# Feed-forward stage: the shared expert's last three down steps moved between the next batch's up steps

## What is computed

```python
shared = jax.nn.silu(x @ shared_w_gate.T) * (x @ shared_w_up.T) @ shared_w_down.T
shared = shared * jax.nn.sigmoid(x @ shared_gate_w.T)
...
out = expert_out + shared
...
x = x + _L0_ffn_ref(_layernorm(x, axis=-1), ...)
```

## Time and profile before

| what | value |
|---|---|
| median of three runs | 855.08 us |
| the profiled execution, its own time | 858.7 us |
| its span | 857.0 us |
| TensorE busy, share of the span | 750.3 us, 88% |
| VectorE busy | 523.9 us, 61% |
| ScalarE busy | 401.4 us, 47% |
| GpSimd busy | 359.9 us, 42% |
| mean granted clock of TensorE | 0.951 |

### The profile page before, as it was taken

How to read it: one execution, slowest core, us unless ns; L and a number is a source line. 1 busy time by engine, 2 the same in 40 slices (tenths; PEclk the granted TensorE clock), 3 DMA queues, 4 the chain that set the end, 5 groups by cost and what they waited for, 6 DMA issues and landing times. The chain is left out here.

```text
span 857.0 us, 16360 instructions
## 1 busy us (share of the span) xinstructions
PE 750.3 (88%) x5618; PEld 569.0 (66%) x5619; DVE 523.9 (61%) x1158; ACT 401.4 (47%) x777; POOL 359.9 (42%) x658
## 2 busy tenths in 40 slices
PE   2589899999999999999887587989679999999997
PEld 1355466575666656666454367868579999988886
DVE  6267777677776768766670349445634445456667
ACT  3116656546655556646556132433435556542232
POOL 4305437283472835625374023767700000057771
PEclk9879999999999999999887868999979999999999
DMA  5659366483755738466111221877645555467864
GB/s 148 236 211 321 143 222 224 167 296 130 250 194 209 261 124 282 138 242 228 61 59 51 86 74 62 301 238 240 239 158 155 181 183 160 134 203 242 265 200 137
DMA packets 102500, 159.67 MB, mean 186 GB/s; under 512 B 7712, under 2 KB 78368, under 8 KB 98208
## 3 DMA queue, kind: packets, MB, share of 16 engines
q1 hardware_dynamic: 96288, 141.99, 49.6%
q0 software_dynamic: 6144, 16.79, 5.7%
HBM read 86.66 MB, written 71.83 MB: 185 GB/s over the span
## 5 line engine op out<-in xcount | busy, mean ns | idle before, releaser
L609 DVE TENSOR_REDUCE neg_max<-ps_w 128x1 f32<-128x512 f32 (+3 forms) x352 | 201.0, 633 | 67.5 <-PE ps_w L711 67.3
L546 ACT ACTIVATE probs<-ps_w 128x512 f32<-128x512 f32 x320 | 167.5, 610 | 32.2 <-PE ps_w L724 31.3
L408 POOL TENSOR_TENSOR pool_scratch<-minus_half 1x1 f32<-1x1 f32 x190 | 34.8, 183 | 263.7 <-ACT probs L546 223.6
L1091 POOL DMA_INDIRECT ex<-yg_dram,slots x64 | 64.5, 1009 | 155.6 <-DMA yg_dram<-y 136.4
L438 POOL TENSOR_SCALAR_AFFINE_SELECT probs<-probs 128x256 f32<-128x256 f32 (+1 forms) x224 | 93.7, 429 | 0.0
L1079 POOL DMA_INDIRECT xg_dram<-srow,slots x64 | 68.0, 1063 | 52.2 <-DVE slots L1242 27.4
L735 PE MATMUL ps_w<-probs,v_aug 128*32 128x512 f32 (+3 forms) x1024 | 81.2, 460 | 5.9 <-POOL probs L438 5.8
L191 PE MATMUL ps_f<-stacks 128*128 128x512 f32 x176 | 72.5, 412 | 12.2 <-DVE xT_lo_f L1260 6.8
L1108 ACT ACTIVATE silu<-ps_f 128x512 f32<-128x512 f32 (+1 forms) x48 | 28.5, 594 | 103.7 <-PE ps_f L193 103.7
L192 PE MATMUL ps_f<-xT_lo_f,stacks 128*128 128x512 f32 x176 | 70.9, 403 | 0.0
L193 PE MATMUL ps_f<-stacks 128*128 128x512 f32 x176 | 70.6, 401 | 0.0
(11 more groups left out here) (167 smaller groups left out, 1839.6 us busy)
## 6 DMA issues: line engine op xcount, KB each, us to landing
qk_dram<-projected SPq DMA_DIRECT2D x96, 256.0 KB, 4.3
stacks<-qk_dram SPq DMA_DIRECT2D x16, 1024.0 KB, 6.1
xg_dram<-zeros SPq DMA_DIRECT2D x20, 512.0 KB, 10.5
srow<-xg_dram SPq DMA_DIRECT2D x40, 256.0 KB, 2.8
q_st<-qk_dram SPq DMA_DIRECT2D x8, 1024.0 KB, 4.8
k_st<-qk_dram SPq DMA_DIRECT2D x8, 1024.0 KB, 8.1
projected<-experts SPq DMA_DIRECT2D x16, 384.0 KB, 4.5
yg_dram<-projected SPq DMA_DIRECT2D x20, 256.0 KB, 2.2
```

Source lines behind the costliest of these rows:

```text
L408: ticks = Ticks(pool, pool_ticks, lambda: pool.tensor_tensor(out=pool_scratch[:, 0:1], in0=minus_half[0:1, 0:1], in1=minus_half[0:1, 0:1], ...
L546: act.activation(probs[:, g, p * PAIR + half * BANK:p * PAIR + (half + 1) * BANK], ps_w[:, plan.bank(kind, which, half), :], ACT.Exp).then ...
L609: dve.tensor_reduce(out=neg_max[u][:, qt, first:first + len(heads)], in_=bank[:, 0:len(heads) * width].rearrange("p (h n) -> p h n", h=len ...
L1091: pool.indirect_dma_start(out=back[:, m, c, :], out_offset=None, in_=yg_rows, in_offset=bass.IndirectOffsetOnAxis(ap=slots[:, c, m:m + 1], ...
```

## The change

Of batches 0, 1, 2 and 4, 5, 6 only down steps 0 to 2 stay behind the batch's own up steps. Steps 3 to 5 stand behind up steps 0, 1 and 2 of the next batch. The four sums of the batch then stand on VectorE behind step 4 of the next batch (`add_down`, `SUMS_BEHIND`), and TensorE's wait for `y_done` keeps its place, ahead of down step 0. The last batch of each half does all its down steps and sums at its end, as before. The low part of the next input (`split_xT`) moves up on both engines to the head of step 6. `x1` gets a second buffer for batches 5 and 7 (`srow[:, 1]`). SyncE stores the sums of batch b-1 and reloads `x1` behind the fifth expert of batch b, or at step 4 of batches 5 and 6. Batch 6's sums aren't stored and read back any more; routed results are added to them in place, and `TILES_BESIDE` moves one tile from batch 4 to batch 7.

```diff
-TILES_BESIDE = {4: (0, 1, 1, 1, 1, 1, 2), ..., 7: (1, 1, 1, 1, 1, 1, 1)}
+TILES_BESIDE = {4: (0, 1, 1, 1, 1, 1, 1), ..., 7: (0, 1, 1, 1, 1, 4, 0)}
+AHEAD = 3
+SUMS_BEHIND = AHEAD + 1
...
+    def x1_of(b):
+        return srow[:, 1] if b > FIRST and b % 2 else x1
...
         def load_x1(b):
-            sp.wait_ge(x1_left, 16 * b)
+            sp.wait_ge(x1_left, 16 * (b if b <= FIRST else b - 1))
...
+        def store_y1(b):
+            sp.wait_ge(y_done, TB * (b + 1))
+            sp.dma_start(item(y1_v, b), x1_of(b)).then_inc(x1_left, 16)
...
         def first_half(b, more):
             load_next_xn(b, more)
             if b == 0:
                 sp.wait_ge(slots_ready, 1)
-            load_x1(b)
+                load_x1(b)
             for e in range(EXPERTS_FROM[b], EXPERTS_FROM[b + 1]):
...
                 if e % 2 and e // 2 < B - 2:
                     rows_of(e // 2 + 2)
-            sp.wait_ge(y_done, TB * (b + 1))
-            sp.dma_start(item(y1_v, b), x1[:, :, :]).then_inc(x1_left, 16)
+                if b and e == EXPERTS_FROM[b] + SUMS_BEHIND:
+                    store_y1(b - 1)
+                    load_x1(b)
+            if not more:
+                store_y1(b)
...
         def second_half(b, more):
-            load_x1(b)
             if b == FIRST:
+                load_x1(b)
+                load_x1(b + 1)
...
+                if FIRST < b < B - 1 and j == SUMS_BEHIND:
+                    store_y1(b - 1)
+                    load_x1(b + 1)
+                    load_y1(b - 1)
...
@@ VectorE @@
+                if j == FT and more:
+                    split_xT(b + 1)
                 if j > 0:
                     dve.wait_ge(h_hi_done, n)
...
-                if j >= 1:
+                if 1 <= j < FT:
                     beside(j - 1)
+                if j == SUMS_BEHIND and b not in (0, FIRST):
+                    add_down(b - 1)
                 if b == 0:
                     routing(j)
+            beside(FT - 1)
...
-            if more:
-                split_xT(b + 1)
             beside(FT)
-            dve.wait_ge(x1_in, 16 * (b + 1))
+            if not more:
+                add_down(b)
...
@@ TensorE @@
             pe.wait_ge(xT_split, (b + 1) * DK)
             for j in range(FT):
-                pe.wait_ge(h_done, b * FT + max(j - 1, 0))
...
+                up(b, j)
...
+                if b not in (0, FIRST) and j + AHEAD < FT:
+                    down(b - 1, j + AHEAD)
...
             pe.wait_ge(y_done, b * TB)
...
-            for j in range(FT):
...
+            for j in range(AHEAD if more else FT):
+                down(b, j)
```

More of the change, by code:

```diff
@@ L908, in build_ffn @@
     stage_in, w_hi_done, w_split = [sem("stage_in0"), sem("stage_in1")], sem("w_hi_done"), sem("w_split")
-    xn_in, x1_in, x1_left = sem("xn_in"), sem("x1_in_f"), sem("x1_left")
+    xn_in, x1_in, x1_left = sem("xn_in"), [sem(f"x1_in_f{n}") for n in range(2)], sem("x1_left")
     xT_ready, xT_hi_done, xT_split = sem("xT_ready"), sem("xT_hi_done"), sem("xT_split")
@@ L952, in fours_loop, with sums_of @@
         four_pairs(TILE_PAIRS - FOUR, False)
+    def x1_of(b):
+        return srow[:, 1] if b > FIRST and b % 2 else x1
+    def sums_of(b):
+        return staged[b % 2] if b < B - 2 else x1_of(b)
     def expert(e, part, lo, hi):
@@ L1420, in ranks, with up, down @@
             pe.matmul(ps[:, COUNT_BANK, :], ones[:, :], flat, start=True, stop=True).then_inc(counts_ready, 1)
+        def up(b, j):
+            pe.wait_ge(h_done, b * FT + max(j - 1, 0))
+            for i in range(2 if j < FT - 1 else 1):
+                col = (2 * j + i) * P
+                for k in range(DK):
+                    at = slice(k * 2 * FF + col, k * 2 * FF + col + P)
+                    last = exact_product(pe, ps[:, 2 + 2 * (j % 2) + i, :], (up_hi[:, at], up_lo[:, at]), (xT_hi[:, k, :], xT_lo[:, k, :]),
+                                         start=k == 0, stop=k == DK - 1)
+            last.then_inc(up_ready, 1)
+        def down(b, j):
+            pe.wait_ge(h_split, b * FT + j + 1)
+            for t in range(TB):
+                last = exact_product(pe, ps[:, 6 + t // 2, (t % 2) * D:(t % 2 + 1) * D],
+                                     tuple(v[0:width(j), j, t * P:(t + 1) * P] for v in (h_hi, h_lo)),
+                                     tuple(v[0:width(j), j * D:(j + 1) * D] for v in (down_hi, down_lo)),
+                                     start=j == 0 and t % 2 == 0, stop=j == FT - 1 and t % 2 == 1)
+                if j == FT - 1 and t % 2:
+                    last.then_inc(down_ready, 1)
         def shared(b, more):
@@ L1442, in shared @@
                 pe.wait_ge(m_y, TILE_PAIRS)
-            for j in range(FT):
[L1444 to L1447, removed]
-                                         tuple(v[0:width(j), j * D:(j + 1) * D] for v in (down_hi, down_lo)),
-                                         start=j == 0 and t % 2 == 0, stop=j == FT - 1 and t % 2 == 1)
-                    if j == FT - 1 and t % 2:
-                        last.then_inc(down_ready, 1)
+            for j in range(AHEAD if more else FT):
+                down(b, j)
         def experts_of(q):
```

52 lines of the change are left out of this document (22 added, 30 removed).

## The result

| | before | after |
|---|---|---|
| median of the runs, us | 855.39 (853.25 to 858.61, 4 runs) | 871.19 (865.81 to 872.72, 4 runs) |
| ratio, 95% interval | | 1.0158 (1.0112 to 1.0204) |
| the profiled execution, us | 858.7 | 871.3 |
| its span, us | 857.0 | 869.6 |
| start of the middle, us | 624.86 | 629.66 |

The changed kernel is slower by 1.6%. (That ratio compares the fast runs of both kernels; the two medians by themselves are 1.8% apart.) The two traces differ by 12.6 us: + 4.8 in the first half, - 0.7 in the middle, + 8.45 in the second half, which begins with batch 4's first up step (752.63 us before, 756.78 after). (The medians differ by 15.8; the profiled execution of before was its slowest one, and I leave the rest to the spread of the executions.)

The account below looks back on a forecast made before the run. Bounds: GpSimd's scatters in the first half, TensorE in the second. The second half's 9.1 us and first half's 1.1 sum to 10.2, which on the 855.08 us median gives 865.3 us; 8-in-10 range 857.5 to 870.

Parts of the forecast that it names:

- the second half: Batches 4 to 7: TensorE is the bound, so new waits, later tail and change of shape cost 9.1 us.
- the first half: Up to the middle's start: 1.1 us later, at 626.0, set by the chain through the last expert's load.
- The wait for the sums in batches 5 and 6: Ahead of down step 0, TensorE waits 2.6 us per batch for VectorE's four sums, 5.2 us in all.
- t: Start of VectorE's product 4 in a batch; sums were forecast from t + 2.24 to t + 3.90.
- The tail of batch 7: From product 4 to the last sums: four more sums and two more tiles on VectorE, 3.7 us more.
- The change of shape: Second half, TensorE: moved steps alternate matmuls of 256 and 512 columns more often, costing 0.2 us.
- The chain: First half's end: expert 13's split, sums, store, last expert's load and splits, batch 3's sums, pair loads; 15.5 us.
- the scatters' gain: First half, GpSimd: by the scatters alone the middle would start 4.9 us earlier; forecast as lost to the chain.
- The scatters decide: Rival, chance 0.22: GpSimd's scatters set the middle's start, 4.9 us earlier; sum + 4.2, 859.3 us.
- The pipeline works: Rival, chance 0.08: sums find TensorE still busy and the first half gains 4.9 us; about 850 us.
- The clock falls behind each new wait: Rival, chance 0.15: slow TensorE stretches add 1.5 us in batches 5 and 6, part in 7; + 3.7, 869.0 us.

Follow-up runs that it names:

- sums5: The changed kernel with the four sums one step later on VectorE, behind product 5 instead of product 4; 985.29 us, ratio 1.0398 to the kernel before.
- sums3: The changed kernel with the four sums one step earlier on VectorE, behind product 3 instead of product 4; 956.84 us, ratio 1.0058 to the kernel before.
- sums3_tiles: The changed kernel with sums behind product 3 and no tile beside the products where sums and low part are due; 952.14 us, ratio 1.0016.
- tiles_again: The kernel of sums3_tiles, unchanged, run again on a third chip; 954.63 us, ratio 0.9995 to the kernel before.
- e15: The changed kernel with the last expert's load ahead of batch 2's store and the `x1` reload; 961.65 us, ratio 1.0126; repeated on a third chip, 968.12 us.
- after_again: The changed kernel, unchanged, run again on the second chip; 961.85 us, ratio 1.0125 to the kernel before.

## Why the prediction was right or wrong

Right in direction and in the main mechanism, short in size: 865.3 us forecast, 871.19 measured, 1.2 us beyond the range's upper end. (By the ratio, 855.08 x 1.0158 gives 868.6, inside it.) Against the trace, 10.2 us forecast and 12.6 measured: the second half came out 0.65 us under its term, the first half 3.7 over.

**The wait for the sums in batches 5 and 6** (forecast 2.6 us each) is 2.23 in each, and a batch took 27.4 us instead of the 27.7 foretold. VectorE's timeline in batch 6 answers to the earlier trace rows:

```profile
824.39 0.69 DVE L1303 TENSOR_TENSOR h<-ps_f,silu 128x512 f32<-128x512 f32 x1 [0.58 <-ACT silu L1124]
...
826.51 1.65 DVE L1329 SCALAR_TENSOR_TENSOR srow<-ps_f,gate,srow 128x256 f32<-128x256 f32 x4
828.20 0.69 DVE L1303 TENSOR_TENSOR h<-ps_f,silu 64x512 f32<-64x512 f32 x1
```

The sums start at t + 2.12 and end at t + 3.8, where I had 2.24 and 3.90. TensorE's side is its timeline at the same place and in batch 7, which answers to the earlier trace rows:

```profile
828.22 0.38 PE L191 MATMUL ps_f<-stacks,h_hi 128*128 128x256 f32 x1 [2.23 <-DVE srow L1329]
828.44 0.28 PE L192 MATMUL ps_f<-w_lo,h_hi 128*128 128x256 f32 x1
...
855.62 0.38 PE L191 MATMUL ps_f<-stacks,h_hi 128*128 128x256 f32 x1 [3.10 <-DVE projected L1329]
855.84 0.28 PE L192 MATMUL ps_f<-w_lo,h_hi 128*128 128x256 f32 x1
```

The step itself is shown by `sums5` and `sums3`: the wait follows the place of the sums. `sums3_tiles` shows that nothing else lengthens a batch by more than 0.1 us.

**The tail of batch 7** (forecast 3.7 us, 10.07 becoming 13.8): product 4 starts at 851.79 and the last four sums at 865.27, 13.48 us; + 3.4. In VectorE's timeline, which answers to the earlier trace rows:

```profile
851.79 0.69 DVE L1303 TENSOR_TENSOR h<-ps_f,silu 128x512 f32<-128x512 f32 x1 [0.58 <-ACT silu L1124]
...
853.91 1.65 DVE L1329 SCALAR_TENSOR_TENSOR projected<-ps_f,gate,projected 128x256 f32<-128x256 f32 x4
...
858.33 3.74 DVE L1335 SCALAR_TENSOR_TENSOR projected<-ex,weight,projected 128x256 f32<-128x256 f32 x8
861.98 3.25 DVE L1335 SCALAR_TENSOR_TENSOR srow<-ex,weight,srow 128x256 f32<-128x256 f32 x8
865.27 1.66 DVE L1329 SCALAR_TENSOR_TENSOR srow<-ps_f,gate,srow 128x256 f32<-128x256 f32 x4
```

VectorE has no idle time between its last products and the end: it is the bound of the tail, as said. TensorE's last matmul starts at 863.98, ahead of it. In these rows eight tiles take 6.94 us, 0.87 each, rather than the 1.03 that I took.

**The change of shape** (0.2 us) is a term that no run shows: a batch of `sums3_tiles` alternates in the same way and takes 25.06 us where the kernel before has 25.03. The two batches and the tail, 2 x 2.35 + 3.4 = 8.1 us, leave 0.35 of the 8.45 without an account. The second half's 9.1 us were 0.65 too many.

**The first half** (forecast + 1.1 us, measured + 4.8) is where the sum failed. The chain was the right one, and the scatters' gain was lost as foretold (4.6 us measured, 4.9 forecast), but I had its terms too small. SyncE's and VectorE's timelines (ScalarE's own split of that expert starts at 621.35):

```profile
612.98 0.38 SPq L993 DMA_DIRECT2D y_dram<-projected  x1
616.26 0.38 SPq L979 DMA_DIRECT2D projected<-x_dram  x1
616.68 0.51 SPq L1003 DMA_DIRECT2D projected<-experts  x1
```

```profile
610.42 0.96 DVE L1351 TENSOR_TENSOR ex<-projected,ex 128x768 fp32r<-128x768 f32 x1
...
622.23 0.96 DVE L1351 TENSOR_TENSOR ex<-projected,ex 128x768 fp32r<-128x768 f32 x1 [6.49 <-ACT ex L1140]
623.82 1.66 DVE L1329 SCALAR_TENSOR_TENSOR projected<-ps_f,gate,projected 128x256 f32<-128x256 f32 x4 [0.63 <-PE ps_f L193]
```

Expert 13's split ended at 611.3, not 610.5: + 0.8. The store took 3.3 us to land instead of 3.1, and the expert's load 4.7 instead of 4.5: + 0.4. SyncE issues the reload of `x1` ahead of the expert, and the store ahead of the pair loads, 0.42 and 0.46 us which the chain left out: + 0.9. The last sums then waited 0.63 us for TensorE, a step that the chain didn't have at all. And the pair loads landed 3.70 us behind their issue where the earlier trace rows had 2.74: + 1.0. (The store of the sums, 512 KB, was issued 0.46 us ahead of them; in the kernel before it was issued at 618.58, 3.40 us ahead. That this is the reason is an argument, not shown.) Together that is 3.7 us, the whole difference between 626.0 and 629.66. Each is small; the step that failed is the sum of the chain "with no slack": 15.5 us from the end of expert 13's split to the middle's start, where it took 18.4. I took its terms from bare landings, without the issue times between them and without TensorE's own steps, and with the landing times of the kernel before.

**The rivals.** *The scatters decide* fell: batch 2's sums ended at 613.0, not before 606. *The pipeline works* fell with the three waits, and `tiles_again` shows what it would have been worth: with the waits taken away it is level with the kernel before; a batch takes as long as before. *The clock falls behind each new wait* fell for the second half: behind 828.22 and 855.62 the matmuls start 0.11 to 0.12 us apart at once. (That "any idle time puts it at risk" is the prediction's own reading of what it takes from the Trainium skill, and these waits of 2.23 us don't bear it out.) It held behind the longer waits of `sums5` (4.6 and 5.5 us), and in batch 3 of the changed kernel, in TensorE's timeline:

```profile
613.00 0.58 PE L191 MATMUL ps_f<-stacks,h_hi 128*128 128x256 f32 x1 [3.10 <-DVE projected L1329]
613.38 0.42 PE L192 MATMUL ps_f<-w_lo,h_hi 128*128 128x256 f32 x1
613.60 0.42 PE L193 MATMUL ps_f<-stacks,h_lo 128*128 128x256 f32 x1
```

From here to 618.7 the matmuls start 0.21 us apart, at a granted clock of 0.50, that is 1.2 GHz; then 0.11 apart. I had written that slow stretches here lie where TensorE isn't the bound. It wasn't by much: the 26 matmuls at half speed took 2.7 us more than the same 26 in `e15` at full speed (5.72 and 3.05 us), of which the last sums felt at most the 0.63.

## What to carry to other kernels

Where an engine is busy for the whole of a batch, a reordering that puts its consumer's work nearer to it can only add waits: count, from one common start, when the one needs the result and when the other has it. The three waits for sums took 7.5 us here, 0.3 with the sums one step earlier and 14.7 one step later; and the time grew by more than the waits once these were long enough for the clock to fall behind them (`sums5`). A chain of transfers with no slack is added up with the issue time of each transfer and of those queued before it, and with landing times taken from rows where as much is under way; and a load that is moved off such a chain wins only the distance to what stands right behind it (in `e15` 3 us at most, not 4).

## What the runs showed of the hardware

- Chips differ by 11 to 12% on this kernel: 855 us on one, 949 to 956 on three others. On those TensorE shows issue waits while GpSimd issues a row of indirect gathers, down to one matmul in 2.80 us, for some 60 us. Holding back each tile's gathers until those of two tiles before had landed gave back 49 us of 955 (`paced2`); three tiles before gave 6 (`paced3`). On the same chips ScalarE has 20 to 59 us of waits up to 655 us whose releaser the profile calls "remote"; on the first it has none.
- A wait of 3.1 us on TensorE is followed by a slow clock in some places and not in others. The changed kernel has both, behind 3.10 us at 613.00 (clock 0.50 for 5.7 us) and at 855.62 (clock 1.00 until 864). In `e15` the same place in batch 3, with 3.12 us, came out without. In `after_again`, with 3.11 us before 630.59, the clock was 1.00 until 631.4 and then 0.51 until 634.9. In `e15_again`, the kernel of `e15` once more, with 3.11 us, ten matmuls started 0.11 to 0.12 us apart, and only at 640.5, 1.25 us behind the wait, did the clock fall, until 643.9:

```profile
639.24 0.39 PE L191 MATMUL ps_f<-stacks,h_hi 128*128 128x256 f32 x1 [3.11 <-DVE projected L1329]
639.46 0.28 PE L192 MATMUL ps_f<-w_lo,h_hi 128*128 128x256 f32 x1
...
640.86 0.42 PE L191 MATMUL ps_f<-stacks,h_hi 128*128 128x256 f32 x1
```

The first matmuls behind a wait, by which I meant to tell, don't tell it all. The Trainium skill (TensorE: Matmul & The Clock Gate, "What's actually happening") says that the monitor behind the clock runs freely, so that the point of change hangs on where the work falls in it; these five waits of 3.10 to 3.12 us, with three outcomes, agree. What length is safe, they can't tell: it stayed at 1.00 behind the waits of 2.23 us in the changed kernel, and was 0.50 to 0.53 behind all three of 4.59 to 5.46 us in the second half of `sums5`.
